# Two states' input products in one POOL operation of 128x2048, in a selective-scan pipeline on one core

## The reference

```python
def step(state, inp):
    x_t, dt_t, k_t, q_t = inp
    dtv = jax.nn.sigmoid(dt_t + dt_head_b)
    dtv = dtv / (1.0 + dtv * jnp.sum(k_t * k_t, axis=-1, keepdims=True))
    kk = k_t * k_t
    state = state * (1.0 - dtv[..., None] * kk[:, None, :]) + (x_t * dtv)[..., None] * k_t[:, None, :]
    y_t = jnp.einsum('bdn,bn->bd', state, q_t)
    return (state, y_t)
```

## Time and profile before

| What | Value |
|---|---|
| runs, median of 3 | 1859.47 us (1859.44 to 1860.31) |
| profiled execution, span from first to last instruction | 1858.7 us |
| PE, PEld busy | 1720.0 us (93%), 1482.7 us (80%) |
| DVE, ACT, POOL busy | 1474.0 us (79%), 1379.3 us (74%), 1369.9 us (74%) |
| `inp`, line 1198, POOL | 256 of 2366 ns |
| `rd`, line 1188, POOL | 256 of 2364 ns |
| `scan`, line 1179, DVE | 1024 of 732 ns |
| chain that ended last, by engine | PE 77%, POOL 7%, issue 7%, DVE 5%, ACT 4% |

### The profile page before, as it was taken

How to read it: one execution, slowest core, us unless ns; L and a number is a source line. 1 busy time by engine, 2 the same in 40 slices (tenths; PEclk the granted TensorE clock), 3 DMA queues, 4 the chain that set the end, 5 groups by cost and what they waited for, 6 DMA issues and landing times.

```text
span 1858.7 us, 34159 instructions
## 1 busy us (share of the span) xinstructions
PE 1720.0 (93%) x12348; PEld 1482.7 (80%) x12348; DVE 1474.0 (79%) x3116; ACT 1379.3 (74%) x2705; POOL 1369.9 (74%) x644
## 2 busy tenths in 40 slices
PE   6788999999999999999999999998776999999998
PEld 5567788887878888887878888787665888899997
DVE  3547888888888888888988888898899678766663
ACT  3468879888887988888798888878643756566664
POOL 0008899898989989898998989898999234444443
PEclk9899999999999999999999999999998999999999
DMA  5011122112122212212221221222122434555552
GB/s 195 1 46 52 64 69 70 61 66 81 50 84 74 70 55 72 81 46 87 75 68 54 75 81 41 92 69 75 57 70 91 136 97 115 136 137 134 136 134 29
DMA packets 69463, 149.86 MB, mean 81 GB/s; under 512 B 5936, under 2 KB 43312, under 8 KB 68912
## 3 DMA queue, kind: packets, MB, share of 16 engines
q1 hardware_dynamic: 57008, 130.90, 20.6%
q0 software_dynamic: 12288, 16.79, 5.2%
HBM read 121.98 MB, written 17.30 MB: 75 GB/s over the span
## 4 chain that ended last, share of the span: by engine, by line
PE 77%; POOL 7%; issue 7%; DVE 5%; ACT 4%; DMA 0%; POOLq 0%; DVEq 0%; ACTq 0%
PE po L1832 9%; PE pD L1130 9%; PE ph L1832 9%; PE pY L1147 9%; PE pA L729 6%; POOL room L1188 3%; PE pA L631 3%; POOL room L1198 3%; PE pB L926 3%; PE pB L936 3%; PE pB L1226 3%; DVE room L1179 2%; PE pA L657 2%; PE pB L957 2%; PE pA L622 2%
## 5 line engine op out<-in xcount | busy, mean ns | idle before, releaser
L1198 POOL TENSOR_TENSOR room<-room 128x1024 f32<-128x1024 f32 x256 | 605.7, 2366 | 171.7 <-DVE room L1113 141.5
L1179 DVE TENSOR_TENSOR_SCAN room<-pD,last,room 128x256 f32<-128x256 f32 x1024 | 691.9, 732 | 49.3 <-PE pD L1130 37.4
L1188 POOL TENSOR_TENSOR room<-room 128x1024 f32<-128x1024 f32 x256 | 605.2, 2364 | 71.5 <-PE pY L1147 70.4
L1160 ACT ACTIVATE room<-room,fixed,kkT 128x512 f32<-128x512 f32 x512 | 406.4, 806 | 55.1 <-PE pD L1130 53.0
L1130 PE MATMUL pD<-fixed,room 128*128 128x128 f32 x2048 | 318.4, 279 | 51.2 <-DVE room L1179 47.1
L1147 PE MATMUL pY<-fixed,room 128*128 128x128 f32 x2048 | 315.9, 278 | 12.0 <-POOL room L1188 12.0
L1130 PEld LDWEIGHTS pD<-fixed,room 128*128 128x128 f32 x2048 | 243.4, 144 | 79.9 <-issue 41.7
L1147 PEld LDWEIGHTS pY<-fixed,room 128*128 128x128 f32 x2048 | 246.9, 144 | 61.0 <-POOL room L1188 25.0
L341 POOL DMA_INDIRECT xg<-xn_rows,W x64 | 67.2, 1050 | 197.1 <-DVE W L335 170.4
L1791 ACT ACTIVATE h<-ph 128x512 f32<-128x512 f32 x128 | 76.7, 599 | 138.0 <-PE ph L1832 100.0
L1832 PE MATMUL po<-w_up,h_up 128*128 128x256 f32 x512 | 149.5, 292 | 3.2 <-DVE h_rest L1699 2.6
(11 more groups left out here) (314 smaller groups left out, 3583.0 us busy)
## 6 DMA issues: line engine op xcount, KB each, us to landing
room<-kq_rows SPq DMA_DIRECT2D x128, 512.0 KB, 4.0
w_in<-w_d SPq DMA_DIRECT2D x32, 1024.0 KB
room<-ndS SPq DMA_DIRECT2D x16, 512.0 KB, 3.2
xt<-x_in SPq DMA_DIRECT2D x16, 256.0 KB, 2.9
y_out<-xo SPq DMA_DIRECT2D x16, 256.0 KB, 2.1
xn_rows<-xnC SPq DMA_DIRECT2D x16, 256.0 KB, 2.2
W<-weights SPq DMA_DIRECT2D x1, 1808.0 KB, 9.4
W<-weights SPq DMA_DIRECT2D x1, 1697.5 KB, 16.7
```

What stands on the lines that cost most here:

```text
L1160: act.activation(decT[:, m % 2, t, :], turn2(ndT, it, NT * DI, t * DI, DI), ACT.Identity, bias=ones_s[:, 0:1], scale=turn2(kkT, it, NT * D ...
L1179: dve.tensor_tensor_scan(run, pD[h][:, k2 * TB:(k2 + 1) * TB], run, last[:, bass.ds(later(it) * (DS * DT) + m * DT + k, 1)], ALU.mult, ALU ...
L1188: pool.tensor_tensor(sq[:, m % 2], st[:, m % 4], kqb[:, m % SLOTS, 1, :].unsqueeze(1).broadcast_to([P, DT, TB]), ALU.mult).then_inc(sem("r ...
L1198: pool.tensor_tensor(st[:, m % 4], turn2(u, it, DT * TB).rearrange("p (k t) -> p k t", k=DT), kqb[:, m % SLOTS, 0, :].unsqueeze(1).broadca ...
```

## The change

POOL makes the input products of states m and m+1, m even, in one operation of 128x2048, at the step where the product of state m stood. The wait for a free slot now covers the slots of both states, so `saved` and `read_out` are asked for up to state m-3 where the single product of state m asked up to m-4. The read-outs stay one per state. An increment of a semaphore that nothing waits for (`st_free`) is dropped. Nothing else is changed.

```diff
-            m = nth(n, "inp", 4)
-            if 0 <= m < DS:
+            p = nth(n, "inp", 8)
+            if 0 <= p < DS // 2:
+                m = 2 * p
                 pool.wait_ge(sem(f"kq_in{m % SLOTS // 2}"), it * (DS // SLOTS * 16) + (m // SLOTS + 1) * 16)
-                if m == 0:
+                if p == 0:
                     pool.wait_ge(sem("u"), it * 2 + 2)
-                pool.wait_ge(sem("saved"), it * DS + m - 3)
-                pool.wait_ge(sem("read_out"), it * DS + m - 3)
-                pool.sem_inc(sem("st_free"), 1)
-                pool.tensor_tensor(st[:, m % 4], turn2(u, it, DT * TB).rearrange("p (k t) -> p k t", k=DT),
-                                   kqb[:, m % SLOTS, 0, :].unsqueeze(1).broadcast_to([P, DT, TB]), ALU.mult)\
-                    .then_inc(sem("inp"), 1)
+                pool.wait_ge(sem("saved"), it * DS + m - 2)
+                pool.wait_ge(sem("read_out"), it * DS + m - 2)
+                pool.tensor_tensor(st[:, m % 4:m % 4 + 2],
+                                   turn2(u, it, DT * TB).rearrange("p (k t) -> p k t", k=DT).unsqueeze(1)
+                                   .broadcast_to([P, 2, DT, TB]),
+                                   kqb[:, m % SLOTS:m % SLOTS + 2, 0, :].unsqueeze(2).broadcast_to([P, 2, DT, TB]), ALU.mult)\
+                    .then_inc(sem("inp"), 2)
```

## The result

| | median of the runs | profiled span | mean granted clock |
|---|---|---|---|
| before | 1859.45 us (1859.32 to 1860.31) | 1858.7 us | 0.979 |
| after | 2178.61 us (2172.54 to 2179.64) | 2176.4 us | 0.929 |

The changed kernel is slower: 1.171 times the time of the one before, 95% interval 1.1694 to 1.1727, or 319 us. The forecast was +210 us, 2069 us, with a range up to 2108. The direction is as forecast and so is the wait that starts the loss; the size lies above the upper end of the range, since a second loss came on top that the forecast did not have.

A forecast was written before the change was run, and what follows sets the result against it. PE was taken to set the pace, with POOL near its limit in the same ring. Thirteen full blocks at 15.0 us (195), block 1 (11) and block 15 (4) gave +210 us on 1858.7: 2069 us, range 1970 to 2108.

The forecast's parts named there:

- POOL's work: Input products on POOL: 256 operations of 128x1024 become 128 of 128x2048, 4.64 us each, bounds 4.36 to 4.75.
- Rival B: POOL's double product is dear, 5.2 us instead of 4.64: 17.8 us per block, about 2108 us; chance 0.07.
- The order: POOL's queue: the double product waits for the read-out directly ahead; a 0.05 us overlap becomes a short wait, inside the bounds.
- The new wait: POOL's double product waits for `saved`; the chain to PE's next sum takes 7.21 us, 15.0 us per block together.
- Hops 3, 4 and 5: Products of states 6/7, 8/9 and 10/11 wait for saved3, saved5 and saved7: +3.6, +2.8 and +2.4 us per block.
- with PE's gaps of today as the measure: The walk through block 9, pricing each wait against PE's gaps in the kernel before: 15.0 us per block.
- hop 2: Product of states 4 and 5 waits for saved1, delaying sum2 on PE: +1.9 us per block.
- long enough for the chain, 0: States 12 and 13: the stretch from sum8 to sum10 on PE holds the chain, so no added time.
- Blocks 1 and 15: Block 1 at an estimated three quarters, 11 us; block 15 with a 1.9 us wait and one more such, 4 us.
- Block 16: Last block, POOL-bound with ACT idle for the most part: 0 us added.
- A: Rival: ACT reaches `saved` earlier while PE stands still; 6 to 10 us per block, about 1970 us; chance 0.18.
- C and D: Rivals: C, POOL's thinner queue closes PE's gaps, 1825 to 1855 us, chance 0.04; D, no change, 1859 us, chance 0.03.

The follow-up runs named there:

- run 7: The changed kernel with `saved` made on DVE by `tensor_reduce` over one element instead of ACT's copy: 1890.97 us, ratio 1.0175.
- run 9: The kernel before with `saved` made on DVE by `tensor_reduce` over one element: 1861.80 us, ratio 1.0015.
- run 4: The changed kernel with `saved` earlier in ACT's queue, at step 17+4m instead of 21+4m: 1909.23 us, ratio 1.0266.
- run 3: The changed kernel with thrown-away matmuls repeated on PE at lines 902 and 957, where PE waited: 2118.09 us, ratio 1.1392.
- run 5: The kernel before with `saved` at step 17+4m instead of 21+4m, nothing else: 1862.58 us, ratio 1.0015.
- run 10: The changed kernel with `saved` at step 17+4m and each double product made by two operations of 128x1024: 1898.59 us, ratio 1.0219.
- runs 6 to 9: `saved` moved to DVE; as a copy, 6 in the changed kernel 2047.19 us, 8 in the kernel before 1962.99 us; 7 and 9 use `tensor_reduce`.

## Why the forecast was right in kind and too small in size

*POOL's work.* Right: 4.48 us from the double product to the read-out behind it (964.03 to 968.51), 4.53 long, inside the bounds of 4.36 and 4.75 and 0.16 below the 4.64 taken. The 4497 ns of the Trainium skill, "GPSIMD Engine Reference", section "Performance versus the Vector engine", was nearer than the 4.64 taken. Rival B, which needed 4.9 us, is out.

*The order.* Right that the wait for the read-out directly ahead costs little: 0.17 us where neighbours overlap by 0.05. Wrong to cost the order at nothing beyond it. In run 7 no product waits for `saved`, and it is 32 us slower than before; 2.5 of them may be DVE's sum (run 9). Of POOL's 9.6 us of idle time per block (83.39 - 73.82), part is in front of read-outs that wait for PE, up to 4.00 us (at 876.58 in that run): a read-out that before had a product behind it to fill POOL's time now has a read-out.

*The new wait.* Right in place and price. From the end of `saved` (963.57 + 0.21) to the sum (970.93) is 7.15 us, 7.21 forecast. Hops 3, 4 and 5 came out within 0.14 us. Run 4 shows that the wait carries the loss: moving `saved` four steps forward returns 269 of 319 us, the clock's share with it.

*The step that failed* is "with PE's gaps of today as the measure". The walk through the block moved PE's work later and left its durations as they were, at 2.4 GHz. PE stood still 1.7 to 4.1 us at each of the five places, and at two of them some 7 us of the work behind ran at 1.2 GHz. In the first, `saved` of state 1 comes later than in the walk by 2.9 us (hop 2); in the second `saved` of state 9, which the forecast had in time ("long enough for the chain, 0"), comes late, and the block ends 3.2 us later. These 6 us times 13 are 79 of the 87 us missing in the full blocks, and the three blocks with more slow work, 3.3 us each, are about the rest. Run 3 shows it by experiment: with work put where PE stood still, and the same waits in the program, 60 us went.

*Blocks 1 and 15.* 11 and 4 us were forecast, 19.5 and 17.2 measured. In block 15 four products besides the first wait for `saved`, by 2.88, 3.44, 5.50 and 6.35 us in POOL's timeline, where "one more such wait" was taken. ACT's share of busy time there (50 of 94 us) says nothing of when a given copy comes up: stage F is still in its queue. The forecast of 4 was a guess at the number of waits, and so was the three quarters for block 1. Block 16, with F gone, was right within 3 us.

*The rivals.* A, the waits absorbed in part, had its argument in ACT getting ahead while PE stands still. ACT did not: three stretches came out as walked and two longer, since its work before those `saved` comes from PE. The forecast's C and D needed `saved` in time; even with it in time (runs 4 and 7) the kernel is slower than before, so its C has nothing to gain from POOL's thinner queue: 128 instructions fewer save POOL 19 us of busy time in a span where PE sets the pace.

Taken together, from the runs: the place of `saved` and the clock loss that follows from it 288 us (after against run 7), of which the clock at least 60 (run 3); POOL's order about 30; the wide operation at most a few us of gain. No run has the order of the kernel before and the wide operation together, so the width is priced only within the new order. No version of the pair beat the kernel before.

## What to carry to other kernels

Joining two operations of an engine that works in order makes the first half ask for what only the second half needed; in a ring of four that took away the one state of slack that hid a small copy. When you find a new wait in front of a nearly full PE, take the idle time from the trace and then ask what clock PE's next stretch will have and who waits for that work. And move a tiny producer (here one number in a table) before changing anything large: it cost 3 us here (run 5), and with its control it tells whether the wait or the operation is at fault.

## What the runs showed that was not expected

- PE waits of 2.19 and 4.05 us were each followed by some 7 us at 1.2 GHz, while waits of 3.38 and 2.52 us in the same block were not; in three of 13 blocks the wait of 3.38 us was, too, and in run 4 even one of 1.63 us (to 906.63). No run here tells which waits cost the clock. Matmuls with thrown-away results made the kernel 60 us faster (run 3).
- A DVE copy of 128x4, 149 ns alone, took up to 4528 ns beside POOL's 128x2048 and up to 2432 beside its 128x1024; `tensor_reduce` on the same elements took 156 in the mean and at most 164 (runs 6 to 9).
- One POOL operation of 128x2048 takes 0.15 us less from start to start than two of 128x1024 (4.48 against 4.63), little for half the instructions: nearly all of POOL's time is elements.
- Blocks of one program differ in steps, by how many slow stretches they hold: 83.7 or 85.3 us in run 10, 102.4 or 105.7 in the changed kernel. Two kernels can differ by 10 us (runs 4 and 10) for this alone, so blocks have to be compared at the same clock.
